# Placing GpSimd's scatters behind other engines' steps, in a fused attention and mixture-of-experts kernel

## The chip, the cores and the metric

The kernel runs on one core of a Trainium2 chip. The metric is the device time in microseconds (us) of one execution, the median of several. The timed runs carry no profile; beside them stands one profiled execution, from which every duration below comes.

## What is computed

Eight images of 64 channels and 256 pixels pass an attention block and then an expert block, both with a residual:

```python
x = x + conv_ref(ln_c(x))        # kq = Wkq x + b (32 channels), v = Wv x + b
                                 # softmax(kq^T kq) over 256 pixels, context, Wo
t = to_tokens(x)                 # 2048 tokens of 64 channels
t = t + ffn_ref(ln_t(t))         # 8 experts, top 2 of a softmax router
# per expert: silu(t W1^T) * (t W3^T), hidden width 682, then W2; weighted by the gates
x = from_tokens(t)
```

All of it is float32.

## The kernel before

The five engines run from queues of their own, written out by hand and tied by semaphores. TensorE multiplies, ScalarE does exponentials, silus and copies out of PSUM, VectorE the statistics, the choice of experts and the products, GpSimd tables, a few small operations and all indirect DMAs, and SP starts the plain DMAs.

**Front.** The images are taken in four pairs (PAIRS), a pair being four tiles of 128 tokens. For an image b, TensorE turns the probabilities (L914) and multiplies them by the values (`attend`, L925), and VectorE makes the new rows in `residual(b)` (L590, L595), which raises `t_ready` to b + 1. Per pair, VectorE then takes the moments (`t_statistics`, L627), GpSimd the inverse deviation (`t_deviation`, L348 and L351), and VectorE chooses experts, computes positions (`positions`) and writes each token's normalised row twice, once for each expert (`normalise_t`, L633, which waits for GpSimd's deviation). VectorE's queue goes on behind it with the maximum of image 2p + 3 (`row_max`, L584), on which ScalarE's exponentials of that image (L452) wait.

**Dispatch.** `scatter_row(p, at)` (L361) is one indirect DMA of 128 rows of pair p into `xs`, which holds the rows of each expert together; a pair needs eight, all of them 32. They count up `dispatched[k]`: pairs 0 and 1 for k = 0, pair 2 for k = 1, pair 3 for k = 2. VectorE computes from the counts, after each of these phases, a table of which expert and which rows each slot of 128 rows takes. SP waits for the table, reads its entries into registers, waits for the dispatch of the phase (`landed`), loads the rows (`load_rows`, L297) and the expert's weights (`load_weights`, L281, 565 KB a slot).

**Expert rounds.** There are NS = 39 slots in NQ = 10 rounds of four (the last has three). In round i, TensorE makes six up steps (L1031 and L1033, two halves of the hidden width's chunk for four slots; the sixth is a narrow tail, L1037), which raise `h3_done` by one each, to 6i + s + 1 after step s; between them stand the turn of the next round's rows (L1013) and of the last round's results (L1073). ScalarE applies the silu to each (L504, L508), VectorE multiplies (L827), and TensorE's down pass follows (L1059). VectorE copies the next rows in `pair_up` (L781, L786) at a round's end and makes tables between the products of rounds 0 and 1. `results(i - 1)` (L839) copies the finished rows of the round before into `y_out`, a ring of four rounds, after product 0 of round i.

**Results.** `scatter_result(j)` (L370) is one indirect DMA of slot j's 128 result rows into `ys`; the first of a round waits for `y_out_ready`. When all 39 have landed, SP and ScalarE load `ys` back, VectorE weighs and TensorE adds and turns the sum.

**GpSimd's order** is the one that the change touches. Behind its tables it runs the deviation of pair 0, then the 32 row scatters pair by pair with the deviations of pairs 1 to 3 set between (pair 1's before the last two scatters of pair 0, pair 2's after pair 1, pair 3's after the second scatter of pair 2), and then the 39 result scatters. Its loops have no waits but those of the helpers. An engine stands at a wait with all that is queued behind it.

Of the kernel before, what the change touches and what calls it, by code (L numbers as in the profile page):

```python
# [16 lines left out]
K_TOP = 2  # L17
# [7 lines left out]
PAIRS = B // 2  # L25
TPP = 2 * TPB
# [5 lines left out]
QUAD = 4  # L32
CAP = B * N
NS = E + (K_TOP * CAP - 1) // SUB
NQ = -(-NS // QUAD)
# [16 lines left out]
STEPS = CHUNKS  # L52
# [9 lines left out]
def metaformer(nc, x_tok, projections, value_output, experts, xs, ys, out):  # L62
    with ExitStack() as ctx:
# [3 lines left out]
        def sem(name):  # L67
            return ctx.enter_context(nc.semaphore(name))
# [118 lines left out]
        attn_done, sum_inverted, t_ready = sem("attn_done"), sem("sum_inverted"), sem("t_ready")  # L187
# [13 lines left out]
        h1_done, h3_done = sem("h1_done"), sem("h3_done")  # L201
# [31 lines left out]
        def pair(p):  # L233
            return slice(TPP * p, TPP * (p + 1))

        def phase_of(p):
            return next(k for k in range(PHASES) if p < KNOWN[k])
# [88 lines left out]
        def _(pool):  # L326
# [19 lines left out]
            def t_deviation(p):  # L346
                pool.wait_ge(moments_t_ready, p + 1)
                nc.gpsimd.tensor_scalar(variance_t[:, pair(p)], moments_t[:, pair(p), 1], EPS[1], None,  # L348
                                        ALU.add).then_inc(variance_t_ready, 1)
                pool.wait_ge(variance_t_ready, p + 1)  # L350
                nc.gpsimd.tensor_tensor(rstd_t[:, pair(p)], variance_t[:, pair(p)], neg_half[:, pair(p)],  # L351
                                        ALU.pow).then_inc(rstd_t_ready, 1)

            def scatter_row(p, at):
                if at % K_TOP == 0:
                    pool.wait_ge(tn_ready, TPP * p + at // K_TOP + 1)
                if at == 0:
                    pool.wait_ge(pos_ready, p + 1)
                    if p == 0:
                        pool.wait_ge(xs_cleared, 16 * QUARTERS)  # L360
                nc.gpsimd.indirect_dma_start(  # L361
                    xs, bass.IndirectOffsetOnAxis(ap=pos[:, p, at:at + 1], axis=0),
                    xrows[:, TPP * p + at // K_TOP, at % K_TOP, :], None).then_inc(dispatched[phase_of(p)], 16)

            def scatter_result(j):
                i, h = divmod(j, QUAD)
                if h == 0:
                    pool.wait_ge(y_out_ready, i + 1)
                    pool.wait_ge(y_row_ready, i + 1)
                nc.gpsimd.indirect_dma_start(  # L370
                    ys, bass.IndirectOffsetOnAxis(ap=y_row[:, j:j + 1], axis=0),
                    y_out[:, i % RING, h, :], None).then_inc(y_scattered[i % RING], 16)
# [32 lines left out]
            add_biases(3)  # L405
            pool.wait_ge(tables_made, TABLES)

            t_deviation(0)
            for p in range(PAIRS):
                for at in range(TPP * K_TOP):  # L410
                    if p == 0 and at == TPP * K_TOP - 2 or p == 2 and at == K_TOP:
                        t_deviation(p + 1)
                    scatter_row(p, at)
                if p == 1:
                    t_deviation(2)
            for j in range(NS):
                scatter_result(j)

        @block.scalar
# [728 lines left out]
```

## Time and profile before

| | us |
|---|---|
| timed runs, median of three | 177.29 |
| timed runs | 174.3, 177.29, 178.6 |
| profiled execution, first to last instruction (its only time) | 238.2 |
| first up step (L1031) | at 68.46 |
| busy: TensorE, VectorE, ScalarE, GpSimd | 166.9, 99.7, 70.8, 85.7 |
| row scatters, L361 | 32 of 987 ns, 31.6 |
| result scatters, L370 | 39 of 960 ns, 37.4 |

The profiled execution is 61 us longer than the median of the timed ones. A row of the timeline has its start, its duration, engine, line, operation, what it writes and reads, and in brackets the idle time of that engine just before it with what ended it; "remote" is a release that the trace can't name, "issue" a stretch in which it shows no wait.

### The profile page before, as it was taken

How to read it: one execution, taken by the hardware profiler on the slowest of the kernel's cores; microseconds unless marked ns; L12 is line 12 of the kernel's file. 1: busy time of each engine (PE TensorE's matmuls, PEld its weight loads, DVE VectorE, ACT ScalarE, POOL GpSimd, SP SyncE). 2: the span in 40 equal slices, each digit the busy share in tenths (PEclk: the TensorE clock that was granted, in tenths of full speed). 3: DMA queues.
4: the chain of work that ended last, by engine and by line, in shares of the span. 5: the costliest groups of instructions: out<-in, count | busy, mean ns of one | idle time of the engine just before them, and what ended most of it. 6: DMA issues, size and time to landing. Idle time of an engine off the chain costs nothing.

```text
span 238.2 us, 4880 instructions
## 1 busy us (share of the span) xinstructions
PE 166.9 (70%) x1682; PEld 139.1 (58%) x1682; DVE 99.7 (42%) x372; ACT 70.8 (30%) x141; POOL 85.7 (36%) x114
## 2 busy tenths in 40 slices
PE   3595957428683069589494994958949697895683
PEld 2364836307452068588393983948839597783543
DVE  2557568255583037584222433223232344342230
ACT  2377433013310034224232142222422323333101
POOL 2963577723277700603205033060230604142400
PEclk9999586555578559979799598895997979798579
DMA  6990000184570229652958075390661600000053
GB/s 185 322 297 20 11 25 22 31 267 151 159 290 23 50 81 328 216 210 46 364 169 313 3 240 196 88 346 4 203 228 42 266 10 14 11 15 11 17 176 91
DMA packets 19893, 33.00 MB, mean 139 GB/s; under 512 B 7691, under 2 KB 13100, under 8 KB 19868
## 3 DMA queue, kind: packets, MB, share of 16 engines
q1 hardware_dynamic: 16732, 29.55, 37.8%
q0 software_dynamic: 2272, 2.35, 3.0%
q10 hardware_dynamic: 864, 0.79, 1.0%
q8 instruction: 14, 0.23, 0.4%
q14 instruction: 11, 0.09, 0.1%
HBM read 25.55 MB, written 7.13 MB: 137 GB/s over the span
## 4 chain that ended last, share of the span: by engine, by line
issue 48%; POOL 21%; PE 11%; DVE 8%; DMA 3%; another core or an unknown queue 3%; ACT 3%; POOLq 1%; SPq 0%; ACTq 0%; DVEq 0%
POOL ys L370 15%; POOL xs L361 5%; PE psum L925 3%; PE psum L914 2%; ACT xn L426 2%; DMA y_in<-ys 2%; DVE rows L595 1%; PE psum L894 1%; PE psum L1103 1%; PE psum L885 1%; DMA ys<-y_out,y_row 1%; DMA proj<-projections 1%; DVE index L606 1%; DVE neg_max L584 1%
## 5 line engine op out<-in xcount | busy, mean ns | idle before, releaser
L370 POOL DMA_INDIRECT ys<-y_out,y_row x39 | 37.4, 960 | 104.0 <-DVE y_out L839 95.2
L827 DVE TENSOR_TENSOR hid<-psum,act_sb 128x512 f32<-128x512 f32 (+1 forms) x50 | 33.4, 676 | 88.9 <-ACT act_sb L504 61.6
L1031 PE MATMUL psum<-x_cols,weights 64*128 64x128 f32 x390 | 52.9, 286 | 13.9 <-issue 12.1
L1031 PEld LDWEIGHTS psum<-x_cols,weights 64*128 64x128 f32 x390 | 47.6, 193 | 19.4 <-issue 15.8
L1033 PE MATMUL psum<-x_cols,weights 64*128 64x128 f32 x390 | 53.1, 286 | 0.9 <-issue 0.9
L504 ACT ACTIVATE act_sb<-psum 128x512 f32<-128x512 f32 (+1 forms) x50 | 28.7, 586 | 70.0 <-remote 42.4
L1033 PEld LDWEIGHTS psum<-x_cols,weights 64*128 64x128 f32 x390 | 47.7, 193 | 1.1 <-issue 1.1
L1059 PE MATMUL psum<-hid,weights 128*64 128x128 f32 x468 | 42.8, 357 | 2.1 <-issue 1.1
L1059 PEld LDWEIGHTS psum<-hid,weights 128*64 128x64 f32 x468 | 39.3, 189 | 4.8 <-issue 2.7
L361 POOL DMA_INDIRECT xs<-xrows,pos x32 | 31.6, 987 | 12.9 <-issue 8.9
L1037 PE MATMUL psum<-x_cols,weights 64*106 64x128 f32 x78 | 8.7, 349 | 23.1 <-ACT act_sb L504 18.4
L1037 PEld LDWEIGHTS psum<-x_cols,weights 64*106 64x106 f32 x78 | 6.1, 208 | 24.7 <-ACT act_sb L504 19.6
L925 PE MATMUL psum<-u_sb,probsT 128*128 128x73 f32 x64 | 13.1, 373 | 5.2 <-issue 4.4
L925 PEld LDWEIGHTS psum<-u_sb,probsT 128*128 128x128 f32 x64 | 12.0, 281 | 7.6 <-issue 5.9
L517 ACT COPY y_cols<-psum 128x256 f32<-128x256 f32 (+1 forms) x10 | 3.6, 362 | 32.3 <-PE psum L1059 32.3
L957 PE MATMUL psum<-ones,before 128*128 128x512 bf16 x24 | 10.0, 562 | 1.8 <-issue 1.8
L452 ACT ACTIVATE probs<-psum,neg_max 128x256 f32<-128x256 f32 x16 | 6.7, 474 | 12.2 <-DVE neg_max L584 12.1
L460 ACT COPY probsT<-psum 128x512 f32<-128x512 f32 x8 | 4.7, 586 | 12.9 <-PE psum L914 8.5
L830 DVE TENSOR_TENSOR hid<-psum,act_sb 42x512 f32<-42x512 f32 x10 | 6.8, 682 | 3.5 <-ACT act_sb L508 3.5
L941 PE MATMUL psum<-taken,before 128*128 128x32 bf16 x4 | 0.7, 181 | 10.5 <-DVE taken L618 10.5
L914 PE MATMUL psum<-ident,probs 128*128 128x128 f32 x32 | 7.9, 395 | 0.3 <-ACT probs L452 0.3
L941 PEld LDWEIGHTS psum<-taken,before 128*128 128x128 bf16 x4 | 0.4, 99 | 13.1 <-issue 13.1
(148 smaller groups left out, 189.9 us busy)
## 6 DMA issues: line engine op xcount, KB each, us to landing
weights<-experts SPq DMA_DIRECT2D x39, 565.0 KB
xs<-zeros SPq DMA_DIRECT2D x4, 1040.0 KB, 11.1
x_in<-xs SPq DMA_DIRECT2D x39, 32.5 KB
ys<-y_out,y_row POOLq DMA_INDIRECT x39
xs<-xrows,pos POOLq DMA_INDIRECT x32
y_in<-ys ACTq DMA_DIRECT2D x2, 256.0 KB, 4.5
y_in<-ys SPq DMA_DIRECT2D x2, 256.0 KB, 4.3
x_sb<-x_tok SPq DMA_DIRECT2D x1, 384.0 KB, 3.4
```

The costliest lines, as they stand in the source:

```text
L361: nc.gpsimd.indirect_dma_start(xs, bass.IndirectOffsetOnAxis(ap=pos[:, p, at:at + 1], axis=0), xrows[:, TPP * p + at // K_TOP, at % K_TOP, ...
L370: nc.gpsimd.indirect_dma_start(ys, bass.IndirectOffsetOnAxis(ap=y_row[:, j:j + 1], axis=0), y_out[:, i % RING, h, :], None).then_inc(y_sca ...
L504: nc.scalar.activation(live(i, act_sb[:, g % 3, :]), live(i, H1_BANK[g % 2]), ACT.Silu).then_inc(silu_done, 1)
L827: nc.vector.tensor_tensor(live(i, hid[:, i % 2, s, :]), live(i, H3_BANK[g % 3]), live(i, act_sb[:, g % 3, :]), ALU.mult).then_inc(hid_done, 1)
L830: nc.vector.tensor_tensor(hid[0:TAIL, i % 2, s, :].rearrange("p (k n) -> p k n", k=2), TAIL_BANKS[0:TAIL], act_sb[0:TAIL, g % 3, :].rearra ...
L914: ins = nc.tensor.transpose(PT_BANK[:, N * j + P * i:N * j + P * (i + 1)], probs[:, b % 2, i, P * j:P * (j + 1)], ident[:])
L925: ins = nc.tensor.matmul(O_BANK[b % 2][:, (TX + 1) * i:(TX + 1) * (i + 1)], probsT[:, b % 2, j, P * i:P * (i + 1)], u_sb[:, 2 * b + j, E:] ...
L957: nc.tensor.matmul(bank[4], before[:], ones[:].unsqueeze(1).to_broadcast([P, BLK // P, P]), start=True, stop=True)
L1031: first_ = nc.tensor.matmul(H1_BANK[g % 2][:, src], weights[0:C, slot, P * s:P * (s + 1)], x_cols[0:C, i % 2, src], start=True, stop=True)
L1033: second_ = nc.tensor.matmul(H3_BANK[g % 3][:, src], weights[C:P, slot, P * s:P * (s + 1)], x_cols[C:P, i % 2, src], start=True, stop=True)
L1037: ins = nc.tensor.matmul(TAIL_BANKS[0:TAIL_W, h % 2, SUB * (h // 2):SUB * (h // 2 + 1)], weights[rows_, slot, TAIL_AT:TAIL_AT + TAIL_W], x ...
L1059: ins = nc.tensor.matmul(Y_BANK[C * (h % 2):C * (h % 2 + 1), P * (h // 2):P * (h // 2 + 1)], weights[:, slot, HP + C * s:HP + C * (s + 1)] ...
```

## The change

The waits of the helpers stay. GpSimd's loops are written out, with more waits:

- pair 0 as before, its deviation of pair 1 still before scatter 6;
- pair 1: scatter 2 waits for the residual of image 4 (`t_ready` 5), scatter 5 for that of image 5;
- pair 2: scatter 3 waits for the residual of image 6, and pair 3's deviation stands before scatter 6 instead of before scatter 2;
- pair 3: scatters 2 to 5 wait for 1, 3, 5 and 6 up steps, scatters 6 and 7 for 7 and 9;
- result scatters: each waits for an up step of its own, in rounds 1 to 9, and the last three are left for the end.

```diff
+            def up_steps(n):
+                pool.wait_ge(h3_done, n)
+
             t_deviation(0)
-            for p in range(PAIRS):
-                for at in range(TPP * K_TOP):
-                    if p == 0 and at == TPP * K_TOP - 2 or p == 2 and at == K_TOP:
-                        t_deviation(p + 1)
-                    scatter_row(p, at)
-                if p == 1:
-                    t_deviation(2)
-            for j in range(NS):
+            for at in range(TPP * K_TOP):
+                if at == 6:
+                    t_deviation(1)
+                scatter_row(0, at)
+            for at in range(TPP * K_TOP):
+                if at == 2:
+                    pool.wait_ge(t_ready, 5)
+                if at == 5:
+                    pool.wait_ge(t_ready, 6)
+                scatter_row(1, at)
+            t_deviation(2)
+            for at in range(TPP * K_TOP):
+                if at == 3:
+                    pool.wait_ge(t_ready, 7)
+                if at == 6:
+                    t_deviation(3)
+                scatter_row(2, at)
+            for at in range(2):
+                scatter_row(3, at)
+            for at in range(2, 6):
+                up_steps((1, 3, 5, 6)[at - 2])
+                scatter_row(3, at)
+            for at in range(6, 8):
+                up_steps((STEPS + 1, STEPS + 3)[at - 6])
+                scatter_row(3, at)
+
+            made = 0
+            for i in range(1, NQ):
+                marks = (2, 4, 5, 6) if i > 3 else (1, 2, 4, 5, 6)
+                if i == 1:
+                    marks = (5, 6)
+                for s in marks:
+                    if made < QUAD * i:
+                        up_steps(STEPS * i + s)
+                        scatter_result(made)
+                        made += 1
+            for j in range(made, NS):
                 scatter_result(j)
```

## Rows read from the trace of the kernel before

**Rows 1.** Timeline of GpSimd: first scatter of the first and ninth burst.
```profile
95.61 0.96 POOL L370 DMA_INDIRECT ys<-y_out,y_row  x1 [12.19 <-DVE y_out L839]
...
211.29 0.96 POOL L370 DMA_INDIRECT ys<-y_out,y_row  x1 [7.91 <-DVE y_out L839]
```

**Rows 2.** Timelines of ScalarE, GpSimd and TensorE in round 5.
```profile
156.30 0.60 ACT L504 ACTIVATE act_sb<-psum 128x512 f32<-128x512 f32 x1 [0.81 <-PE psum L1031]
...
158.72 0.96 POOL L370 DMA_INDIRECT ys<-y_out,y_row  x1 [0.31 <-issue]
160.78 1.08 ACT L504 ACTIVATE act_sb<-psum 128x512 f32<-128x512 f32 x2 [3.88 <-remote]
...
162.55 5.27 PE L1059 MATMUL psum<-hid,weights 128*64 128x128 f32 x48
```

**Rows 3.** Timeline of TensorE, end of round 0 and start of round 1.
```profile
89.18 0.60 PE L1037 MATMUL psum<-x_cols,weights 64*106 64x128 f32 x8
89.71 2.84 PE L1059 MATMUL psum<-hid,weights 128*64 128x128 f32 x48
92.48 0.37 PE L1031 MATMUL psum<-x_cols,weights 64*128 64x128 f32 x1
...
94.47 0.37 PE L1031 MATMUL psum<-x_cols,weights 64*128 64x128 f32 x1
```

**Rows 4.** Timeline of TensorE in round 0.
```profile
68.46 0.41 PE L1031 MATMUL psum<-x_cols,weights 64*128 64x128 f32 x1 [0.25 <-issue]
...
72.28 0.37 PE L1031 MATMUL psum<-x_cols,weights 64*128 64x128 f32 x1
...
74.33 0.39 PE L1033 MATMUL psum<-x_cols,weights 64*128 64x128 f32 x2 [0.89 <-issue]
85.72 0.58 PE L1031 MATMUL psum<-x_cols,weights 64*128 64x128 f32 x1 [11.00 <-issue]
```

**Rows 5.** Busy time by stretch: PE, PEld, DVE, ACT, POOL, granted clock, DMA share, GB/s.
```profile
65.70:83.50 17.80, 6.75 (x60) 4.64 (x58) 6.92 (x33) 1.18 (x2) 13.74 (x14) 0.69 0.33 117
```

**Rows 6.** Timelines of four engines during pair 1's scatters.
```profile
40.57 1.06 PE L914 MATMUL psum<-ident,probs 128*128 128x128 f32 x4
...
44.09 0.59 ACT L460 COPY probsT<-psum 128x512 f32<-128x512 f32 x1 [4.48 <-issue]
...
44.73 1.99 PE L925 MATMUL psum<-u_sb,probsT 128*128 128x73 f32 x8 [3.10 <-issue]
...
47.02 0.96 POOL L361 DMA_INDIRECT xs<-xrows,pos  x1 [0.30 <-issue]
...
49.91 0.17 DVE L590 RECIPROCAL inv_sum<-psum 128x2 f32<-128x2 f32 x1 [6.74 <-remote]
```

**Rows 7.** Timelines of four engines, from pair 1's third scatter to image 7's transpose.
```profile
40.70 0.96 POOL L361 DMA_INDIRECT xs<-xrows,pos  x1 [0.30 <-issue]
...
42.00 0.49 DVE L595 SCALAR_TENSOR_TENSOR rows<-psum,inv_sum,x_base 128x72 f32<-128x72 f32 x2
...
52.17 1.04 POOL L351 TENSOR_TENSOR rstd_t<-variance_t,neg_half 128x4 f32<-128x4 f32 x1
...
54.45 1.11 DVE L633 TENSOR_SCALAR xrows<-rows,moments_t,rstd_t 128x128 f32<-128x128 f32 x4
55.47 0.68 DVE L584 TENSOR_REDUCE neg_max<-psum 128x2 f32<-128x512 f32 x1
...
56.44 0.85 ACT L452 ACTIVATE probs<-psum,neg_max 128x256 f32<-128x256 f32 x2
...
58.40 1.06 PE L914 MATMUL psum<-ident,probs 128*128 128x128 f32 x4
```

**Rows 8.** Timeline of SP: loads of the first two rounds' rows.
```profile
58.01 3.94 SPq L297 DMA_DIRECT2D x_in<-xs  x8
```

**Rows 9.** Timeline of VectorE: the copies of the next rows.
```profile
65.44 0.42 DVE L781 COPY x_pairs<-x_in 128x512 f32<-128x512 f32 x1
...
71.22 0.42 DVE L781 COPY x_pairs<-x_in 128x512 f32<-128x512 f32 x1
```

## Prediction

> **What bounds the kernel now.** I began with the two times that don't agree. The profiled execution spans 238.2 us; the three timed runs have a median of 177.29 us. No other time of the profiled execution is given, so every duration below stands against 238.2 us, and it must first be explained where 61 us go that a timed run doesn't have. The chain of waits helps little: it follows GpSimd's scatters, with "issue" between them for 48% of the span.
>
> The timeline of GpSimd shows nine bursts of four result scatters and a last one of three, one per round of the experts (a round is four slots, six up steps and one down pass). The first burst starts at 95.61, the ninth at 211.29 [rows 1], so a round lasts (211.29 - 95.61) / 8 = 14.46 us. The timelines of the other engines in round 5 show the inside of one: the burst's fourth scatter ends at 159.68. ScalarE's silu of 156.30 is the last one on time; the next comes at 160.78, 1.1 us after the burst has ended, and behind 3.88 us that the trace puts down to nothing it can name ("remote"). TensorE, idle until then, does its 48 down records in 5.27 us [rows 2]. With no burst before it the same 48 records took 2.84 us [rows 3]. So a burst costs its round some 3 us of stall, and up to 2.4 us more in a down pass at the lower of the two clock levels.
>
> The same shape stands in the front. While GpSimd runs 14 row scatters between 65.7 and 83.5 [rows 5], TensorE halts inside one up step, where no instruction has a wait, from 74.7 to 85.72 [rows 4]. During pair 1's scatters ScalarE starts at 44.09 what TensorE had ready at 41.63 (2.4 us late), and VectorE starts at 49.91 a residual whose matmuls ended at 46.72 (3.2 us late), just after the last of those scatters ends at 47.98 [rows 6].
>
> **Are these stalls in the timed runs?** I add them up. Front: 2.4 + 3.2 = 5.6. Round 0: its first up step is at 68.46, that of round 1 at 92.48, 24.0 us; without the halt I get 10.1 (3.8 to the third step at 72.28, which waited for VectorE's tables and the second turn, three up steps of 0.95, tail 0.6, down 2.84), so 13.9 is stall [rows 3, 4]. A steady round without stall: up step 0 with its two turns 1.99 (92.48 to 94.47), four up steps of 0.9 to 1.05, tail 0.6, down 2.84, sum 9.05 to 9.6 [rows 3] (a step's 16 records follow each other by 0.108 in pairs, 0.87 us; what is over that is the silu that gates it, my estimate). Eight rounds: 8 x (14.46 - 9.6) = 38.9, or 43.3 by 9.05, less about 2.0 for the table arithmetic that VectorE really does in rounds 1 and 2. Round 9 I take at 3. Sum 5.6 + 13.9 + 36.9 + 3 = 59.4, or 63.8 by the short round. A run without any of it lasts 238.2 - 59.4 = 178.8, or 174.4. The timed median, 177.29, lies between. **So the stalls belong to the profiled execution, and a timed run holds at most some 3 us of them.** The forecast stands on this reading.
>
> The Trainium skill (NOTIFIC — the notification-queue block, Overflow) says that the block which carries trace records never drops one inside its own pipeline but holds the producers back; no row here shows that block. By that rule a timed run would have none of the stalls, which is where the sum above comes out. The skill (SBUF — State Buffer, Who interferes with whom) also says that TensorE and ScalarE never wait for another engine's port; both do halt beside scatters here, so by that rule the cause isn't a port.
>
> **The change, part by part.**
> (a) *Result scatters, one per up step.* 39 stay 39, each 0.96 us. Their new waits are met by TensorE's own up steps. Round 1 issues two, rounds 2 and 3 five each, later rounds four, at steps 2, 4, 5 and 6, so from round 4 on each round issues the four of the round before. The last three wait for the last y_out as before: the tail starts at the same place. Nobody waits for the earlier ones but the ring of four y_out buffers, filled again four rounds (38 us) later: cost 0. What spreading can save in a timed run is the residue: 177.3 - 174.4 = 2.9 us, by the other end nothing. The middle of the two ends is 176.6; I take 0.7 as the gain.
> (b) *Pair 3's row scatters behind up steps.* Before, these eight ran in one go after VectorE's rows. Now six wait for up steps, the last for the ninth, two steps and a turn into round 1. Their landing is asked for by SP for round 4's rows, after the third table, which VectorE finishes behind step 3 of round 1 and which round 4 needs three rounds later: cost 0.
> (c) *Pair 2's scatters.* Before, two ran, then GpSimd stood until pair 3's moments and the other six followed. Now six run and only two follow. SP's loads for rounds 2 and 3 then wait for the table alone, but VectorE takes these rows after the last step of round 0: 0, at best a gain of 0.5.
> (d) *Pair 1's scatters wait for the residuals of images 4 and 5.* This one lies on a path. GpSimd has one queue, and behind these eight stands the deviation of pair 2 (1.4 us), for which VectorE waits, in order, before its rows, its maximum of image 7 and so ScalarE's exponentials of image 7. I take the trace's times and leave out the 5.6 us of stall. Before: last scatter ends at 47.98, deviation 48.1 to 49.5, rows at 49.6 (VectorE would be there at 54.45 - 5.6 = 48.9). After: scatter 2 starts not at 40.70 but when the residual of image 4 ends, 42.6: 1.9 us late. That of image 5 is then no wait: its matmuls end at 46.72 - 2.4 = 44.3, and GpSimd reaches scatter 5 at 46.4. The eight end at 49.9, the deviation at 51.5, the rows start at 51.6 instead of 49.6, the maximum ends 1.7 later at 53.3 instead of 51.3, the exponentials at 54.2 instead of 52.2. TensorE's transpose of image 7 stood at 58.40 - 5.6 = 52.8, behind the attention of image 6; so 0.6 us are covered and **1.4 us** are late from there to the first up step [rows 6, 7]. Bounds: 0, if a timed run has the residual of image 4 by 1.9 us earlier; 2.0, if the cover is gone. SP waits for the landing of pair 1's rows too, and issued its loads of them at 58.01, or 52.4 without stall, by when even the later scatters are over [rows 8]; VectorE copies the first of them at 65.44, or 59.8 [rows 9]. Cost 0, and what is late next is this copy if the landing slips by over 4 us.
>
> Sum: 177.3 + 1.4 - 0.7 = **178.0**.
>
> **The rivals.** *Faster: the stalls are in the timed runs, smaller.* Then my unstalled round is too long, and each of nine bursts gives back, say, 0.7 us and the front 1: 177.3 + 1.4 - 7.3 = 171.4. It passes 2% (3.5 us, about what a measurement of this kernel can tell from no change) from 4.9 us of relief. For it: the timed runs differ by 4.3 us among themselves, so something in them is irregular. Against it: the sum above leaves 2.9 us. 18%.
> *Slower: VectorE's copies meet the scatters.* The last scatter of a round now starts with the tail step, just where VectorE copies the next rows (L781), for which the next turn waits; the burst used to lie at steps 1 to 4. If that copy is held for a scatter, it costs up to 0.96 us in each of eight rounds, 7.7 us, and with (d) gives 186.4; it decides from 0.26 us a round on. Against it: beside a scatter (one ran from 71.00) the copy took 0.42 us, as with GpSimd idle [rows 9], so by rows it is 0. The page on SBUF has, in the same section, the rule that such a float32 copy and a GpSimd instruction can lock each other out for the whole instruction; the row shows no such wait. 14%, larger sizes of (d) with it.
> *No change at all:* (d) is covered and no residue is there, 177.3. With the forecast that is 68%, with a range of its own of 175 to 180.5.
>
> **Numbers.** Likeliest 178. The range of 173 to 181.5 leaves out the deeper part of each rival, about one case in five. Faster 0.18, same 0.68, slower 0.14.
>
> **What would show it.** In the profile of the changed kernel ScalarE's idle times named "remote" shrink or go, rounds last 9.4 to 12 us and the span falls to between 185 and 215 us, while the timed median hardly moves: this is the step most worth checking. Pair 1's third scatter starts right behind VectorE's residual of image 4, and VectorE waits some 2 us for pair 2's deviation. The copies at L781 stay at 0.42 us. The forecast is wrong if the timed runs fall along with the span (the stalls are real there), or rise by over 3.5 us (then look at the copies first, and at SP's wait for pair 1).

## The result, and the profile after

The timed runs of the changed kernel have a median of 176.23 us (174.93 to 178.78, 20 runs), those of the kernel before 176.3 us. The ratio is 1.0058, with a 95% interval of 1.003 to 1.0085, so the change costs 0.6%, about 1.0 us. (The ratio leaves out the executions that fell into a slower state; that is why it says more than the two medians, which take all of them in.) The forecast was 178.0 us, no change within 2%.

The profile changed far more than the time. Its span fell from 238.2 us to 174.4 us, 1.9 us under its own execution's time of 176.32 us. The first lines of the page of the changed kernel:

```profile
span 174.4 us, 4884 instructions
...
PE 145.1 (83%) x1682; PEld 121.7 (70%) x1682; DVE 100.1 (57%) x372; ACT 71.4 (41%) x141; POOL 86.5 (50%) x114
...
PE   0669949578787699997998999999999999984672
...
PEclk9999996955555558999999999999999999999699
```

TensorE is busy in 83% of it, and in nine tenths or more of every slice from the 23rd to the 35th. By stretch (columns as in [rows 5]), 50 us in the middle of the rounds show no idle TensorE and the full granted clock:

```profile
100.00:150.00 50.00, 50.00 (x795) 46.42 (x793) 27.23 (x51) 24.84 (x45) 22.79 (x23) 1.00 0.73 250
```

The timelines of GpSimd, ScalarE and TensorE of the changed kernel in one round, against [rows 1, 2]: four scatters stand apart, the silus follow each other with 0.3 us between, and the down pass takes 2.84 us, which [rows 3] had only in the round that no burst preceded.

```profile
125.30 0.96 POOL L370 DMA_INDIRECT ys<-y_out,y_row  x1 [3.86 <-PE psum L1065]
126.93 0.96 POOL L370 DMA_INDIRECT ys<-y_out,y_row  x1 [0.67 <-PE psum L1065]
...
126.64 0.60 ACT L536 ACTIVATE act_sb<-psum 128x512 f32<-128x512 f32 x1 [0.35 <-PE psum L1063]
127.53 0.60 ACT L536 ACTIVATE act_sb<-psum 128x512 f32<-128x512 f32 x1 [0.29 <-PE psum L1063]
...
127.91 2.84 PE L1091 MATMUL psum<-hid,weights 128*64 128x128 f32 x48
```

A round lasts 8.97 us there (the first waited scatters of two rounds, at 116.33 and 125.30). The front shows step (d). In its timelines of VectorE, GpSimd and TensorE, the residual of image 4 ends at 41.88 and the third scatter of pair 1 starts at 42.16, and VectorE then waits 2.02 us for the deviation of pair 2 and TensorE 0.59 us for the exponentials of image 7, against [rows 7]:

```profile
41.39 0.49 DVE L627 SCALAR_TENSOR_TENSOR rows<-psum,inv_sum,x_base 128x72 f32<-128x72 f32 x2
42.16 0.95 POOL L361 DMA_INDIRECT xs<-xrows,pos  x1 [1.54 <-DVE rows L627]
...
49.79 1.04 POOL L351 TENSOR_TENSOR rstd_t<-variance_t,neg_half 128x4 f32<-128x4 f32 x1
50.87 1.12 DVE L665 TENSOR_SCALAR xrows<-rows,moments_t,rstd_t 128x128 f32<-128x128 f32 x4 [2.02 <-POOL rstd_t L351]
...
53.51 1.12 PE L946 MATMUL psum<-ident,probs 128*128 128x128 f32 x4 [0.59 <-ACT probs L484]
```

Taken alone, the two spans would say that the change removes 64 us of stalls from a profiled execution. The experiments speak against it.

### The profile page after: what moved, and what is told of

It reads as the page before. It is cut to its first block, busy times and chain, and to the rows that moved or that the text cites. A ratio compares the mean times of both kernels' runs of the same rounds, so it can differ in the third digit from the quotient of the medians.

```text
span 174.4 us, 4884 instructions
## 1 busy us (share of the span) xinstructions
PE 145.1 (83%) x1682; PEld 121.7 (70%) x1682; DVE 100.1 (57%) x372; ACT 71.4 (41%) x141; POOL 86.5 (50%) x114
## 4 chain that ended last, share of the span: by engine, by line
PE 48%; DVE 11%; DMA 11%; SPq 8%; issue 8%; POOL 6%; ACT 4%; POOLq 1%; DVEq 0%; ACTq 0%
PE psum L1063 17%; PE psum L1091 10%; DMA weights<-experts 6%; PE psum L957 4%; POOL xs L361 3%; PE psum L946 3%; POOL ys L370 2%; ACT xn L458 2%; DMA y_in<-ys 2%; PE psum L1135 2%; SPq L281 2%; SPq L285 2%; SPq L289 2%; PE psum L1045 2%; SPq L297 2%
## 5 line engine op out<-in xcount | busy, mean ns | idle before, releaser
L370 POOL DMA_INDIRECT ys<-y_out,y_row x39 | 38.1, 977 | 44.2 <-PE psum L1065 35.8
L1063 PE MATMUL psum<-x_cols,weights 64*128 64x128 f32 x390 | 50.8, 283 | 1.0 <-DMA weights<-experts 0.8
L1065 PE MATMUL psum<-x_cols,weights 64*128 64x128 f32 x390 | 50.9, 284 | 0.0
L1063 PEld LDWEIGHTS psum<-x_cols,weights 64*128 64x128 f32 x390 | 46.9, 192 | 5.1 <-issue 2.9
L1065 PEld LDWEIGHTS psum<-x_cols,weights 64*128 64x128 f32 x390 | 46.9, 192 | 0.0
L536 ACT ACTIVATE act_sb<-psum 128x512 f32<-128x512 f32 (+1 forms) x50 | 29.3, 587 | 25.8 <-PE psum L1063 25.8
L1091 PE MATMUL psum<-hid,weights 128*64 128x128 f32 x468 | 28.8, 276 | 0.2 <-DVE hid L859 0.2
L1091 PEld LDWEIGHTS psum<-hid,weights 128*64 128x64 f32 x468 | 25.9, 137 | 2.0 <-DVE hid L859 0.5
L528 ACT COPY x_cols<-psum 128x512 f32<-128x512 f32 (+1 forms) x10 | 5.7, 575 | 6.6 <-PE psum L1045 6.4
L989 PEld LDWEIGHTS psum<-ones,before 128*128 128x128 bf16 x24 | 2.8, 131 | 7.9 <-issue 7.7
L458 ACT ACTIVATE xn<-x_sb,shift_x,rstd 128x64 f32<-128x64 f32 x16 | 5.7, 429 | 6.0 <-DVE std L601 6.0
L1069 PE MATMUL psum<-x_cols,weights 64*106 64x128 f32 x78 | 6.5, 281 | 1.3 <-DVE hid L859 1.3
```

What stands on the lines that cost most here:

```text
L370: nc.gpsimd.indirect_dma_start(ys, bass.IndirectOffsetOnAxis(ap=y_row[:, j:j + 1], axis=0), y_out[:, i % RING, h, :], None).then_inc(y_sca ...
L458: ins = nc.scalar.activation(xn[:, p, i, m, :], x_sb[:, t, :], ACT.Identity, bias=shift_x[:, t:t + 1], scale=rstd[:, t:t + 1])
L536: nc.scalar.activation(live(i, act_sb[:, g % 3, :]), live(i, H1_BANK[g % 2]), ACT.Silu).then_inc(silu_done, 1)
L989: nc.tensor.matmul(bank[4], before[:], ones[:].unsqueeze(1).to_broadcast([P, BLK // P, P]), start=True, stop=True)
L1063: first_ = nc.tensor.matmul(H1_BANK[g % 2][:, src], weights[0:C, slot, P * s:P * (s + 1)], x_cols[0:C, i % 2, src], start=True, stop=True)
L1065: second_ = nc.tensor.matmul(H3_BANK[g % 3][:, src], weights[C:P, slot, P * s:P * (s + 1)], x_cols[C:P, i % 2, src], start=True, stop=True)
```

## The experiments

"First up step" below is counted from VectorE's first rows of pair 0 (L633 before, L665 after), since the loads at the start differ by up to 1.5 us from one execution to the next.

**Which part does what (e1 to e4).** e1 keeps the front of before and spreads the results; e2 has the changed front and the results in bursts:

```diff
 # e1: the changed loop of result scatters, the front of before
-            for j in range(NS):
-                scatter_result(j)
+            ... marks and up_steps(STEPS * i + s) as in the change
 # e2: the changed front, and behind it
+            for j in range(NS):
+                scatter_result(j)
```

> The front's order of before, the result scatters one per up step as in the changed kernel. Theory A (the stalls beside GpSimd's bursts exist in the profiled execution alone): timed 0.995 to 1.000 of before (176.3 us), since nothing is moved on a path and at most a small residue is given back; the span of the profiled execution falls by the rounds' share of the stalls (8 x (14.46 - 9.0) = 44, and 3 of the last round) from 238 to about 191 us, and keeps the halt of round 0 and the 5.6 us of the front. Rival B (the stalls are in the timed runs too, smaller): timed 0.96 to 0.985. Rival C (the copies at a round's end meet the last scatter): timed 1.01 or more.

> The changed front (pair 1 behind the residuals, pairs 2 and 3 spaced), the result scatters in bursts of four as before. Theory A: timed 1.005 to 1.009 of before, all of what the changed kernel loses (the 1.4 us that VectorE waits for pair 2's deviation), and a span of 238 - 5.6 - 13.9 + 1.4, about 220 us, with rounds of 14 us. Rival B: timed below 1.00, because the halt of round 0 goes. If the loss is made in the rounds, this one is at 1.00.

e1 measured 0.998 of before (0.9935 to 1.0025), e2 0.9987 (0.9937 to 1.0038). Their spans were 175.1 and 175.2 us. Neither theory A nor rival B had that. A expected 191 and 220, since each kernel kept a part of the bursts; B expected at most 0.985 of e1, whose interval ends above that. e1 has the row scatters of before in one go and no halt of round 0. In e2 the result bursts are there and nothing halts: its first three bursts are in place at 80.65 (behind the last row scatter), 89.31 and 98.28, one every 9 us.

```profile
89.31 0.96 POOL L370 DMA_INDIRECT ys<-y_out,y_row  x1 [3.92 <-DVE y_out L861]
90.58 0.96 POOL L370 DMA_INDIRECT ys<-y_out,y_row  x1 [0.30 <-issue]
91.84 0.96 POOL L370 DMA_INDIRECT ys<-y_out,y_row  x1 [0.30 <-issue]
93.10 0.96 POOL L370 DMA_INDIRECT ys<-y_out,y_row  x1 [0.30 <-issue]
98.28 0.95 POOL L370 DMA_INDIRECT ys<-y_out,y_row  x1 [4.22 <-DVE y_out L861]
```

So the theory "a profiled execution stalls at every burst" fell with these two. e2's timed ratio also missed the 1.005 that A expected of the front alone; that is taken up below. e3 takes pair 1's waits out of the changed kernel, e4 keeps them and moves the deviation:

```diff
 # e3
-                if at == 2:
-                    pool.wait_ge(t_ready, 5)
-                if at == 5:
-                    pool.wait_ge(t_ready, 6)
 # e4: the waits stay, and in pair 1
+                if at == 6:
+                    t_deviation(2)
                 scatter_row(1, at)
-            t_deviation(2)
```

> The changed kernel without its two waits in pair 1 (t_ready 5 and 6), all else as changed. Theory A: VectorE waits 2 us less for pair 2's deviation, timed 1.4 us (0.8%) below the changed kernel, 0.996 to 1.000 of before; the profiled span may grow by up to 5.6 us where pair 1's scatters run together again. If the waits cost nothing in a timed run (the residual of image 4 is there early), it equals the changed kernel, 1.005.

> The changed kernel with its waits, but the deviation of pair 2 set before pair 1's scatter 6 instead of behind scatter 7. Its input is there at 46.03 in the changed kernel's trace and scatter 5 ends at 46.9, so VectorE finds it at 48.7 with no wait (it waited 2.02 us). Theory A: the 1.4 us come back though the scatters are as late as in the changed kernel: timed 0.996 to 1.000 of before. If the loss comes from late rows (SP's loads of them) and not from the deviation, it stays at 1.005.

Timed 0.9998 (0.9957 to 1.0039) and 1.0004 (0.9943 to 1.0064), spans 174.4 and 174.1 us. The times alone don't reach far at these intervals; the traces do. The same two lines of VectorE's timeline and TensorE's first up step, in e3:

```profile
25.68 1.11 DVE L661 TENSOR_SCALAR xrows<-rows,moments_t,rstd_t 128x128 f32<-128x128 f32 x4
...
49.79 1.11 DVE L661 TENSOR_SCALAR xrows<-rows,moments_t,rstd_t 128x128 f32<-128x128 f32 x4 [0.89 <-POOL rstd_t L351]
...
62.88 0.54 PE L1059 MATMUL psum<-x_cols,weights 64*128 64x128 f32 x1 [0.25 <-ACT x_cols L524]
```

and in e4:

```profile
25.07 1.10 DVE L666 TENSOR_SCALAR xrows<-rows,moments_t,rstd_t 128x128 f32<-128x128 f32 x4
...
48.19 1.11 DVE L666 TENSOR_SCALAR xrows<-rows,moments_t,rstd_t 128x128 f32<-128x128 f32 x4
...
62.20 0.58 PE L1064 MATMUL psum<-x_cols,weights 64*128 64x128 f32 x1 [0.25 <-ACT x_cols L529]
```

VectorE waits 0.89 us in e3 and not at all in e4, and the first up step comes at 37.20 and 37.13 us, against 38.10 in the changed kernel (63.64 - 25.54). So the whole change costs 0.9 us up to there. The first 0.9 us of VectorE's wait cost nothing: that is the cover, TensorE's attention of image 6 by the prediction's account.

The spans of these two executions don't show the loss. From the first up step to the last instruction e3 takes 111.5 us and the changed kernel 110.8, though one of its middle rounds takes 9.8 us instead of 8.97. What makes up for it are TensorE's last turns. In e3 they ran at a granted clock of 0.70 in the mean:

```profile
165.83 5.37 PE L1131 MATMUL psum<-ident,weighted 128*128 128x128 f32 x32 [1.39 <-DVE weighted L897]
```

in the changed kernel at 1.00:

```profile
167.38 3.84 PE L1135 MATMUL psum<-ident,weighted 128*128 128x128 f32 x32 [1.03 <-DVE weighted L901]
```

So the traces show the loss as far as the first up step, and only the timed ratios show it in the whole.

**Is it the kernel or the execution? Double the burst (e5 to e8).** e5 is the kernel before, unchanged. e6 holds back all of pair 1, e7 is before with bursts of eight, e8 is e4 with another order in SP's queue.

```diff
 # e6, in the changed kernel
-                if at == 2:
-                    pool.wait_ge(t_ready, 5)
-                if at == 5:
+                if at == 0:
                     pool.wait_ge(t_ready, 6)
 # e7, in the kernel before
             for j in range(NS):
+                if j % (2 * QUAD) == 0 and j < 8 * QUAD:
+                    pool.wait_ge(y_out_ready, j // QUAD + 2)
                 scatter_result(j)
 # e8, in e4: SP
-                    load_rows(i, at)
-                    load_weights(i, owners_of(i))
+                    if i + 1 in own:
+                        load_rows(i + 1, rows_of(i + 1))
+                    load_weights(i, owners_of(i))
```

> The kernel before, profiled once more. The spread results (e1) and the changed front alone (e2, with bursts of four kept) both had spans of 175 us, so the bursts by themselves don't stall a profiled execution. Theory A' (the 238 us were one disturbed execution, not what a profile does to bursts): the span is 172 to 177 us, rounds last 9.0 us, bursts of four in them, no idle time named remote. Theory A (a profile stalls every burst): the span is near 238 us again with rounds of 14.5 us. In either case it gives the front of before undisturbed or not: under A' VectorE's wait for pair 2's deviation is 0.3 to 0.7 us, where the changed kernel has 2.02.

> The kernel before with its result scatters in bursts of eight every second round (rounds 2, 4, 6, 8) instead of four in each; the last seven as before. It doubles the length of a burst, about 10 us. If bursts cost the timed runs nothing: 0.995 to 1.005 of before, rounds of 9.0 us. If a burst holds other engines in a timed run from some length on, as it did in the 238 us execution from its second scatter on: four bursts of 3 to 6 us of halts, 1.07 or more.

The kernel before, profiled a second time, spans 174.9 us (176.64 us timed). Lines of its page, one line by stretch, and VectorE's row behind its wait for pair 2's deviation:

```profile
span 174.9 us, 4880 instructions
...
PE 146.6 (84%) x1682; PEld 122.4 (70%) x1682; DVE 100.4 (57%) x372; ACT 71.7 (41%) x141; POOL 85.8 (49%) x114
...
PE   0669849748788699996999999999989999983882
...
100.00:150.00 50.00, 49.19 (x776) 45.49 (x774) 26.58 (x50) 24.02 (x43) 20.27 (x22) 1.00 0.74 248
...
50.32 1.12 DVE L633 TENSOR_SCALAR xrows<-rows,moments_t,rstd_t 128x128 f32<-128x128 f32 x4 [1.26 <-POOL rstd_t L351]
```

The span is the one that A' expected. VectorE's wait for pair 2's deviation is not: 1.26 us, where 0.3 to 0.7 was expected (0.88 in e7, which has the same front). Bursts of four stand in it, and beside one (105.68 to 110.43) silus and down pass run as in the changed kernel:

```profile
105.68 0.96 POOL L370 DMA_INDIRECT ys<-y_out,y_row  x1 [4.25 <-DVE y_out L839]
106.94 0.96 POOL L370 DMA_INDIRECT ys<-y_out,y_row  x1 [0.31 <-issue]
108.21 0.96 POOL L370 DMA_INDIRECT ys<-y_out,y_row  x1 [0.30 <-issue]
109.47 0.96 POOL L370 DMA_INDIRECT ys<-y_out,y_row  x1 [0.30 <-issue]
...
106.58 0.60 ACT L504 ACTIVATE act_sb<-psum 128x512 f32<-128x512 f32 x1 [0.30 <-PE psum L1031]
107.53 0.60 ACT L504 ACTIVATE act_sb<-psum 128x512 f32<-128x512 f32 x1 [0.35 <-PE psum L1031]
108.42 0.60 ACT L504 ACTIVATE act_sb<-psum 128x512 f32<-128x512 f32 x1 [0.30 <-PE psum L1031]
...
108.80 2.84 PE L1059 MATMUL psum<-hid,weights 128*64 128x128 f32 x48
```

e7 measured 0.9955 of before (0.9912 to 0.9998), span 174.4 us, though GpSimd issued for 10 us on end in every second round. So even a burst of eight costs nothing that was measured, timed or profiled, and rival B of e1 falls with it. What held the engines in the 238.2 us execution beside its scatters doesn't come from this kernel's program alone: the same program has it in one profiled execution and not in another. What it was stays open, as it didn't come again in 13 further profiled executions of this kernel and its variants. Whether it was the chip, the profiler or something else on the machine isn't shown.

> The changed kernel with pair 1's scatters held back as a whole: scatter 0 waits for the residual of image 5 (44.98 in the changed kernel's trace), and no other wait in that pair. The path of the prediction's part (d), enlarged: the eight end at 54.9, the deviation at 56.3, VectorE's rows start at 56.4 instead of 50.87 and all of these 5.5 us reach the first up step: 69.1 instead of 63.6, timed 1.035 to 1.04 of before. If the rounds have slack that takes a late start back (SP's loads, which the rounds wait for in places), it is less: 1.02 to 1.03. If the deviation is on no path, 1.006.

e6 measured 1.0304 (1.02 to 1.0408), 5.4 us. VectorE's timeline and the first up step:

```profile
25.79 1.11 DVE L663 TENSOR_SCALAR xrows<-rows,moments_t,rstd_t 128x128 f32<-128x128 f32 x4
...
56.74 1.12 DVE L663 TENSOR_SCALAR xrows<-rows,moments_t,rstd_t 128x128 f32<-128x128 f32 x4 [7.68 <-POOL rstd_t L351]
...
69.52 0.58 PE L1061 MATMUL psum<-x_cols,weights 64*128 64x128 f32 x1 [0.25 <-ACT x_cols L526]
```

The rows start at 30.95 behind pair 0's instead of 25.33, 5.6 us later, and the first up step at 43.73 instead of 38.10, 5.6 us later. Past the cover, the path through the deviation passes every microsecond on: 43.73 - 37.20 = 6.5 us against before's order at the same clock, 5.4 us in the timed ratio, with an interval of 3.5 to 7.2. The 1.035 to 1.04 that was expected lies above the measured 1.0304, but inside its interval, and so does the whole of the lower band.

> The kernel of e4 (pair 2's deviation before pair 1's scatter 6), and SP issues each round's row loads before the weights of the round before them. In e4's and the changed kernel's traces VectorE's copy at a round's end waits up to 2.7 us for these rows, and one round lasts 9.9 us instead of 8.97. With the rows early the waits for x_in in the rounds go and each round lasts 8.97: 0.9 us less than e4 in the rounds, timed 0.990 to 0.997 of before. If the late weights are what binds, or SP's own pace, it is 1.00.

e8 missed: 1.019 (1.0114 to 1.0265). The copies at a round's end no longer wait for x_in, as meant, but SP issues the weights of round 2 at 77.37, behind two rounds of rows. That is 13.95 us behind the first up step (63.42), where in e4 it is 9.51 us (71.71 behind 62.20). TensorE waits for them at the start of round 2:

```profile
68.66 6.24 SPq L297 DMA_DIRECT2D x_in<-xs  x8
77.37 6.31 SPq L281 DMA_DIRECT2D weights<-experts  x8
...
87.52 0.55 PE L1066 MATMUL psum<-x_cols,weights 64*128 64x128 f32 x1 [2.60 <-DMA weights<-experts]
```

This order of SP's queue costs time there; no other was tried.

**The cost again, with what takes it away beside it (e9 to e12).** e9 is the changed kernel, e10 is e3, e11 is e4. e12 is the kernel before with one edit:

```diff
-                    if p == 0 and at == TPP * K_TOP - 2 or p == 2 and at == K_TOP:
+                    if p < 2 and at == TPP * K_TOP - 2 or p == 2 and at == K_TOP:
                         t_deviation(p + 1)
                     scatter_row(p, at)
-                if p == 1:
-                    t_deviation(2)
```

> The changed kernel once more, beside the two kernels that take its loss away. The traces put the first up step 0.9 us later than without pair 1's waits (38.10 against 37.20 us behind VectorE's first rows, both at a granted clock of 0.91 to 0.92 around 30 us): timed 1.003 to 1.008 of before, and 0.4% to 0.9% above e10 and e11. If the first measurement's 1.0058 was chance: 0.998 to 1.002.

> e3 once more (the changed kernel without pair 1's two waits): 0.997 to 1.001 of before, if these waits are all that the change costs.

> e4 once more (the waits kept, pair 2's deviation before scatter 6): 0.997 to 1.001 of before, as e10, if the loss runs through the deviation and not through late rows.

> The kernel before with pair 2's deviation moved before pair 1's scatter 6, nothing else. VectorE's wait for it (1.26 us in e5) goes. By the cover that the prediction names (TensorE turns image 7 behind the attention of image 6) nearly nothing of it reaches the first up step: 0.996 to 1.001 of before. Without that cover it would be 0.993.

| run | edit | timed, of before | rows of pair 2 | first up step | clock, 28 to 34 us |
|---|---|---|---|---|---|
| changed | | 1.0058 (1.003 to 1.0085) | 25.33 | 38.10 | 0.92 |
| e9 | changed, again | 1.0079 (1.004 to 1.0118) | 25.31 | 38.07 | 0.98 |
| e3 | no waits in pair 1 | 0.9998 (0.9957 to 1.0039) | 24.11 | 37.20 | 0.91 |
| e10 | the same, again | 0.9977 (0.9914 to 1.0039) | 25.54 | 39.09 | 0.50 |
| e4 | deviation early | 1.0004 (0.9943 to 1.0064) | 23.12 | 37.13 | 0.95 |
| e11 | the same, again | 1.0011 (0.9965 to 1.0057) | 23.18 | 37.19 | 0.95 |
| e12 | before, deviation early | 0.9979 (0.9933 to 1.0025) | 23.13 | 37.19 | 0.97 |
| e7 | front of before | 0.9955 (0.9912 to 0.9998) | 24.09 | 37.18 | 0.90 |
| e5 | before, again | one run only | 25.02 | 37.79 | 0.68 |
| e2 | changed front alone | 0.9987 (0.9937 to 1.0038) | 26.29 | 39.06 | 0.67 |
| e1 | front of before | 0.998 (0.9935 to 1.0025) | 25.54 | 39.08 | 0.50 |

The loss came again: 1.0058 and 1.0079, both intervals above 1, while both ways of taking it out lie at 1 within their intervals, in two measurements each. The intervals of e4 and e11 reach to 1.0064 and 1.0057, so the timed runs alone don't separate them from the changed kernel. What does is the first up step: e4 and e11 keep the waits and the late scatters and have it at 37.13 and 37.19, the changed kernel at 38.10 and 38.07. So the loss as far as that step runs through the deviation. The changed kernel lies 1.0% above e10, a little over what was expected, and 0.7% above e11. e12 came out as expected, and beats neither e11 nor before by anything that can be measured: the wait that it removes was covered.

The last column sorts the traces. Of those at 0.90 or more, the front of before (e7) and e3 have the first up step at 37.18 and 37.20, the changed one at 38.10 and 38.07. At 0.67 and 0.68 the changed front (e2) is at 39.06 and before (e5) at 37.79, 1.3 us apart. e2's timed ratio, 0.9987, doesn't show these 1.3 us. Its interval reaches to 1.0038, 0.7 us, and so leaves out both ratios of the changed kernel, whose front is the same. That stays open, and it is the one measurement against the account given here.

## Why the prediction was right, and where it was not

**The time.** 178.0 was forecast from a median of 177.29 of three runs; 176.23 came, with a cost of 1.0 us against before's 176.3 of twenty. Forecast as a difference: +0.7 us; measured: +1.0 (0.5 to 1.5). The sum behind it was +1.4 for (d) and -0.7 for spreading. The first was too large and the second isn't there, so that two errors in part cancel; how close the difference came is partly luck.

**Are the stalls in the timed runs?** The sum that took them out of the 238.2 us gave 174.4 to 178.8 us for an execution without them. e5 spans 174.9 us. Its parts were close too: a round of 9.05 to 9.6 us (8.97 measured, just below), first up step at 68.46 - 5.6 = 62.9 (63.09 in e5), round 0 of 10.1 us (63.09 to 73.30 in e5, 10.2). The sum has a slip: 174.4 to 178.8 are spans, and were set against a timed median, while e5's span is 1.7 us under the time of the same execution. The residue of 2.9 us, of which 0.7 was taken as a gain, is by that some 1.2 us.

**That step's other half failed.** The prediction said that "a burst costs its round some 3 us of stall", in a profiled execution, and that spreading would shrink the stalls and let the span fall to 185 to 215 us. The span did fall, to 174.4, and a reader of the two pages alone would call the mechanism shown. e2, e5 and e7 speak against it: profiled bursts of four and of eight with no stall. The fall of the span was not made by the change, since the kernel before has it too. One profiled execution was disturbed, in step with GpSimd's scatters, and the prediction took what one execution showed for a property of profiles. The forecast survived because it kept the stalls out of the timed runs for another reason, the arithmetic against the timed median.

**(a) Result scatters apart.** Cost 0 held: in e1 and the changed kernel the rounds take 9.0 us, and the last three scatters begin 0.64 us after VectorE begins their y_out, as before (0.63 us in e5). The gain of 0.7 us, taken as the middle of a residue, isn't to be seen: e1 is at 0.998 with 1 in its interval, and e7, which does the opposite, at 0.9955 with an interval that ends just below 1.

**(b), (c) Pair 3 and pair 2.** Cost 0 held: the first up step of e3, which has both, is that of e7, which has neither, to 0.02 us. Behind it, where pair 3's scatters now lie, the last down pass starts 88.92 us after the first up step in e3 (62.88 to 151.80) and 88.96 us in e7 (62.89 to 151.85).

**(d) Pair 1's waits.** The step that carries the result. The mechanism was right in each link that the traces show: the third scatter behind the residual of image 4, the wait of VectorE (forecast 2.7 us against 0.7 before; 2.02 against 0.88 in e7, at nearly the same clock), part of it covered by TensorE. The size was forecast at 1.4 us; it measured 0.9 us in the traces at the higher clock, 1.3 at the lower, 1.0 and 1.4 timed. The mis-sized term is the delay of the scatters. It was 1.9 us in the disturbed trace; in the changed kernel the third one starts 1.24 us after the 40.92 at which it could have (39.66 + 0.95 + 0.31). Counted from VectorE's first rows, the residual of image 4 ends at 16.3 us there (41.88 - 25.54) and at 18.0 in the disturbed trace (42.49 - 24.53). The cover was smaller too: VectorE's rows of pair 2 come 1.22 us later than in e3 and the first up step 0.90, so 0.3 were covered, where the forecast had 0.6 of 2.0.

**The rivals.** Faster (the stalls are real) fell with e1, e5 and e7. Slower (VectorE's copies meet the scatters): all ten copies of the changed kernel take 0.41 to 0.56 us, those of e5 0.42 to 0.55, so their median cost is 0. The Trainium skill (SBUF — State Buffer, Who interferes with whom) says that such a copy and a GpSimd instruction can lock each other out, and that the one that issues first holds the shared ports for its whole instruction. One result scatter of the changed kernel took 1.70 us where the others take 0.96, and a copy of VectorE ran inside it.

```profile
102.55 1.70 POOL L370 DMA_INDIRECT ys<-y_out,y_row  x1 [0.32 <-issue]
...
102.98 0.41 DVE L813 COPY x_pairs<-x_in 128x512 f32<-128x512 f32 x1
```

The copy began second and took no longer than elsewhere, so the longer one is the scatter that began first, which the rule as told doesn't give. Four other result scatters of this trace have such a copy beside them and take 0.96 us. That the copy is what made the one longer isn't shown; its round was no longer for it (8.97 us). The Trainium skill's rule on records that hold their producers back (NOTIFIC — the notification-queue block, Overflow) is left where it was: 14 profiled executions show no hold but the 238.2 us one, whose cause is open.

## What to carry to other kernels

Before explaining a profile, compare its span with the timed runs; where they differ by a third, profile the unchanged kernel again, since here one execution had 60 us of halts that the next one didn't have. Before delaying work on an in-order queue, look at what stands behind it for another engine: here eight scatters could wait for nothing, but the small operation behind them could not, and with it two scatters earlier the delay no longer reached the first up step. A wait that is partly covered costs nothing up to the cover and everything beyond it (here 0.9 us free, and 5.6 of 5.6 us from the changed kernel to e6).

## What the runs showed of the hardware that was not expected

The front's length goes with TensorE's granted clock near 30 us, which changes from one execution to the next. At 0.91 in that stretch (e3) VectorE's rows of pair 1 come 10.8 us behind those of pair 0; at 0.50 (e10, the same program) 12.7 us, and the first up step at 39.09 instead of 37.20. 0.50 is the lower of the clock's two levels, 1.2 of 2.4 GHz, for the whole stretch. Before it fell the engine was busy for 2.43 us of the four from 20 to 24 us in e3 and for 1.73 in e10; from 24 to 28 us the granted clock was 0.71 and 0.50, and in e3 alone it had risen again by 28 to 34 us. These 1.9 us are twice what the change costs. The timed runs differ in the clock too: of e10's twelve, the four with a mean granted clock of 0.86 took 177.2 to 178.0 us, the two with 0.89 took 174.0. In which stretch they lost it isn't on record. The stretches in e3 (columns as in [rows 5]):

```profile
20.00:24.00 4.00, 2.43 (x19) 1.38 (x18) 3.51 (x24) 2.32 (x8) 0.54 (x2) 1.00 0.02 5
24.00:28.00 4.00, 2.74 (x15) 2.23 (x15) 3.19 (x15) 2.46 (x8) 1.95 (x2) 0.71 0.00 0
28.00:34.00 6.00, 4.96 (x33) 3.57 (x33) 3.46 (x23) 2.06 (x5) 4.57 (x5) 0.91 0.11 31
```

and in e10:

```profile
20.00:24.00 4.00, 1.73 (x13) 0.76 (x12) 3.62 (x26) 2.33 (x8) 1.26 (x2) 0.96 0.01 2
24.00:28.00 4.00, 3.36 (x17) 2.87 (x18) 2.98 (x12) 2.31 (x7) 1.73 (x3) 0.50 0.03 8
...
28.00:34.00 6.00, 6.00 (x30) 4.78 (x29) 1.99 (x13) 1.62 (x4) 4.30 (x5) 0.50 0.09 25
```
